# The tanh of a u tile written to its place in SBUF instead of back into its bank

## The reference

```
proj = hidden_states @ W_in.T
u, gate = split(proj, 2, axis=-1)                   # 2048 channels each
u = silu(causal_conv(u, conv_w, 4 taps) + conv_b)
ssm_p = u @ Wx.T  ->  dt, B, C, each normed
delta = softplus(dt @ Wdt.T + dt_bias)
state = exp(delta * A) * state + (delta * u) * B    # over 512 steps, 16 states a channel
y = (sum over states of state * C + u * D_param) * silu(gate)
x = layernorm(x + y @ W_out.T)
```

## Time and profile before

| what | value |
|---|---|
| median of 3 runs | 2404.43 us (2392.73 to 2404.64) |
| the profiled execution's own time | 2413.77 us |
| its span (first to last instruction) | 2412.0 us |
| busy: TensorE | 2168.1 us (90%) |
| busy: VectorE | 2090.4 us (87%) |
| busy: GpSimd | 1802.3 us (75%) |
| busy: ScalarE | 1495.7 us (62%) |
| mean granted TensorE clock | 0.933 of 2.4 GHz |

### The profile page before, as it was taken

One profiled execution on the slowest core, in us unless ns is written; L12 is line 12 of the kernel. 1 busy time (PEld: TensorE's weight loads), 2 busy tenths in 40 slices (PEclk: granted clock), 3 DMA queues, 4 the chain that ended last, 5 costly groups with the idle time before them and its releaser, 6 DMA issues.

```text
span 2412.0 us, 30712 instructions
## 1 busy us (share of the span) xinstructions
PE 2168.1 (90%) x10528; PEld 1591.5 (66%) x10528; DVE 2090.4 (87%) x2462; ACT 1495.7 (62%) x2133; POOL 1802.3 (75%) x769
## 2 busy tenths in 40 slices
PE   8998688797879979989989998989999998898987
PEld 6767567576755547778875566767875567665555
DVE  4558899999989999999989998999969998999732
ACT  4388677676665565667676667665586568565421
POOL 4378889799689987967768986887678986588500
PEclk9989789899879988999989999989999999898999
DMA  4466566455323334666443434465463335353313
GB/s 149 138 211 214 188 212 198 140 195 179 101 66 95 109 113 141 210 213 199 158 158 107 108 118 132 138 230 170 134 195 98 108 114 183 107 169 104 82 57 122
DMA packets 152651, 353.52 MB, mean 147 GB/s; under 512 B 17776, under 2 KB 27376, under 8 KB 152496
## 3 DMA queue, kind: packets, MB, share of 16 engines
q1 hardware_dynamic: 152496, 351.56, 45.8%
HBM read 282.65 MB, written 68.85 MB: 146 GB/s over the span
## 4 chain that ended last, share of the span: by engine, by line
PE 50%; DVE 27%; issue 9%; ACT 7%; POOL 2%; DVEq 0%; ACTq 0%; POOLq 0%
PE state_t L767 13%; DVE drive L906 13%; PE bank L816 13%; DVE y_acc L914 6%; PE bank L793 5%; PE bank L795 5%; PE bank L794 5%; DVE scratch L921 2%; PE bank L767 2%; ACT decay L1142 2%; POOL drive L1307 1%; ACT L1142 1%; DVE ln_stats L989 1%; PE bank L861 1%; ACT rows L1244 1%
## 5 line engine op out<-in xcount | busy, mean ns | idle before, releaser
L1307 POOL TENSOR_TENSOR drive<-delta_u,b_bcast 128x2048 f32<-128x2048 f32 x256 | 1170.5, 4574 | 154.7 <-PE state_t L767 152.8
L906 DVE TENSOR_TENSOR_SCAN drive<-decay,drive 128x512 f32<-128x512 f32 x1024 | 1193.1, 1204 | 73.6 <-ACT decay L1142 50.3
L1142 ACT ACTIVATE decay<-delta,a_sb 128x512 f32<-128x512 f32 x1024 | 692.9, 688 | 394.2 <-DVE drive L906 390.0
L767 PE MATMUL state_t<-identity,drive 128*128 128x128 f32 x4096 | 618.9, 292 | 163.8 <-DVE drive L906 120.6
L767 PEld LDWEIGHTS state_t<-identity,drive 128*128 128x128 f32 x4096 | 510.9, 150 | 375.3 <-DVE drive L906 175.7
L793 PE MATMUL bank<-cols_high,w_split 128*128 128x512 f32 (+1 forms) x1280 | 551.8, 431 | 13.0 <-POOL w_split L1332 8.7
L914 DVE SCALAR_TENSOR_TENSOR y_acc<-state_t,c_rows,y_acc 128x512 f32<-128x512 f32 x711 | 506.2, 735 | 63.3 <-PE state_t L767 60.2
L795 PE MATMUL bank<-cols_high,w_split 128*128 128x512 f32 (+1 forms) x1280 | 513.7, 401 | 0.0
L794 PE MATMUL bank<-cols_low,w_split 128*128 128x512 f32 (+1 forms) x1280 | 512.6, 400 | 0.0
L816 PE MATMUL bank<-channels,w_raw 128*128 128x512 f32 x960 | 454.7, 598 | 0.0
L1312 POOL TENSOR_TENSOR y_acc<-y_acc,scaled 128x512 f32<-128x512 f32 x249 | 319.7, 1284 | 180.0 <-ACT scaled L1162 178.2
(11 more groups left out here) (154 smaller groups left out, 1424.9 us busy)
## 6 DMA issues: line engine op xcount, KB each, us to landing
w_split<-w_split SPq DMA_DIRECT2D x288, 512.0 KB, 3.8
b_bcast<-b_rows SPq DMA_DIRECT2D x256, 256.0 KB, 3.5
w_raw<-in_w_out SPq DMA_DIRECT2D x128, 256.0 KB, 2.9
w_raw<-in_w_in SPq DMA_DIRECT2D x96, 256.0 KB, 4.2
gates<-scratch SPq DMA_DIRECT2D x64, 256.0 KB, 3.8
scratch<-gates SPq DMA_DIRECT2D x64, 256.0 KB, 4.5
rows<-in_x_rows SPq DMA_DIRECT2D x4, 2048.0 KB, 8.6
out<-rows SPq DMA_DIRECT2D x16, 512.0 KB, 4.9
```

The lines of the kernel that those rows point to most:

```text
L767: last = engine.transpose(bank[0:tile.shape[1], i * P:(i + 1) * P], tile, identity[:, :])
L906: engine.tensor_tensor_scan(state, decay[(GT * s + t) % DECAYS][:, :], state, 0.0, ALU.mult, ALU.add).then_inc(signal["scan"])
L1142: engine.activation(decay[i % DECAYS][:, :], delta[:, g % 2, t, :], ACT.Exp, scale=a_sb[:, j, n:n + 1]).then_inc(signal["decay"])
L1307: engine.tensor_tensor(drive[key % DRIVES][:, :, :], du[:, :, :], row, ALU.mult).then_inc(signal["drive"])
```

## The change

The tanh of a u tile is written to the place in `channels` where u will stand, and u_silu reads it there and writes over it. The bank is given back after u_conv instead of after u_silu. The wait for the out product of sequence b-2 moves from u_silu (VectorE) to u_tanh (ScalarE), since that is now the first to write the tile. The planner's assumed duration of u_silu is 0.6 instead of 0.585.

```diff
@@ u_job, the planner's pieces @@
-        put("DVE", due + 3.5, 2.18, "u_conv", key, [("u_tap", key)])
-        put("ACT", due + 4, 0.53, "u_tanh", key, [("u_conv", key)])
-        put("DVE", due + 4.5, 0.585, "u_silu", key, [("u_tanh", key)] + ([("o_mm", (b - 2, h, DT - 1)) for h in range(HT)] if b > 1 else []),
-            give=[("bank", ("u_mm", key)), ("scratch", ("u", key))])
+        put("DVE", due + 3.5, 2.18, "u_conv", key, [("u_tap", key)], give=[("bank", ("u_mm", key))])
+        put("ACT", due + 4, 0.53, "u_tanh", key, [("u_conv", key)] + ([("o_mm", (b - 2, h, DT - 1)) for h in range(HT)] if b > 1 else []))
+        put("DVE", due + 4.5, 0.6, "u_silu", key, [("u_tanh", key)], give=[("scratch", ("u", key))])
@@ VectorE @@
-                    conv, bank = scratch[place["scratch", ("u", key)]], banks[place["bank", ("u_mm", key)]]
+                    u, conv = chan[b % 2][:, j, :], scratch[place["scratch", ("u", key)]]
                     e.wait_ge(*done("u_tanh", key))
-                    if b > 1:
-                        for h in range(HT):
-                            e.wait_ge(*done("o_mm", (b - 2, h, DT - 1)))
-                    engine.scalar_tensor_tensor(chan[b % 2][:, j, :], bank[:, :], 1.0, conv[:, :], ALU.add, ALU.mult).then_inc(signal["u_silu"])
+                    engine.scalar_tensor_tensor(u, u, 1.0, conv[:, :], ALU.add, ALU.mult).then_inc(signal["u_silu"])
@@ ScalarE @@
                 elif stage == "u_tanh":
+                    b, j = key
                     e.wait_ge(*done("u_conv", key))
-                    engine.activation(banks[place["bank", ("u_mm", key)]][:, :], scratch[place["scratch", ("u", key)]][:, :], ACT.Tanh).then_inc(signal["u_tanh"])
+                    if b > 1:
+                        for h in range(HT):
+                            e.wait_ge(*done("o_mm", (b - 2, h, DT - 1)))
+                    engine.activation(chan[b % 2][:, j, :], scratch[place["scratch", ("u", key)]][:, :], ACT.Tanh).then_inc(signal["u_tanh"])
```

## The result

The changed kernel takes 2480.6 us (median of 4 runs, 2475.6 to 2488.1) against 2404.5 for the kernel before: a ratio of 1.0335, 95% interval 1.0309 to 1.0361, 3.35% or 80 us slower by the ratio; the two medians are 76 us apart.

A forecast was written before the change was run, and what follows sets the result against it. TensorE and VectorE, waiting for each other, bound the kernel. Stalls 72, less 14 hidden, plus 5 clock, less 4 early bank, plus 1.5 for two more VectorE additions, gave 60 us on 2404.4: 2464 us, range 2428 to 2506.

The forecast's parts named there:

- What bounds: Whole kernel: TensorE (90% busy) and VectorE (87%) wait for each other; VectorE has 29.05 us idle in the three stretches.
- the stretches: 300 to 640, 1030 to 1200 and 1598 to 1720 us, where the 48 touched tiles of sequences 1 to 3 run.
- The second input: u_silu on VectorE, sequences 1 to 3: two SBUF inputs make it wait for GpSimd's instruction; 72 us, 61 to 84.
- Lost rounds: u_silu beside busy GpSimd: a stopped instruction can also wait through GpSimd's next one; 9 us for 34 tiles.
- What idle time hides: VectorE in the three stretches: idle time swallows 14 us of the waits, half of 29.
- The clock: TensorE: idle in long stalls, its clock falls and work after runs slower; 5 us more, 0 to 18.
- The early bank: TensorE's waits for a u tile's bank: release after the third convolution step gains 4 us, 0 to 8.2.
- The order: All engines: the new plan hardly moves the order, 12 out products go behind a last transpose; 0, with 12 us either side.
- The sum: Whole kernel: 72 - 14 + 5 - 4 + 1.5 = 60 us slower, predicted median 2464 us.
- Hidden stalls (A): Rival, VectorE's stalls hidden in its idle time: within 0.5% of before, 2407 us at 40 us of waits; chance 0.08.
- No stall (B): Rival, u_silu does not stop and the earlier bank is what is left: faster, 2387 us; chance 0.08.
- Stalls that breed stalls (C): Rival, most of the 34 u_silus lose another GpSimd round and TensorE's clock stays low: 2522 us; chance 0.07.

The follow-up runs named there:

- the run with half the dose: Kernel before, its order; only odd tiles have their tanh in SBUF and a u_silu with two SBUF inputs: 2434.9 us, ratio 1.0129.
- the operands alone: Kernel before, every engine's order unchanged; tanh goes to SBUF, u_silu reads two SBUF inputs, out-product wait moves too: 2473.1 us, ratio 1.0296.
- the late release: Changed kernel's order with the old operands; whoever takes the bank next waits for u_silu: 2441.1 us, ratio 1.0159.
- the memset run: Changed kernel, order and early bank release kept; u_silu's product replaced by a VectorE memset of the tile: 2428.9 us, ratio 1.0106.

## Why the prediction was right

- **What bounds.** Right. In the stretches VectorE was full, and what u_silu took there came out as length: 50.7 us more of u_silu, 46 us more of stretch. In the first 110 us u_silu stalled as well, 17.8 us for 16 tiles instead of 11.0, and the first scan began at 140.3 us in both.
- **The second input.** The mechanism was right in each part: 0.67 us where GpSimd is idle, the rest of the drive otherwise. The size was off for the changed kernel. I took 72 us (61 to 84); it measured 50.7, under my lower end. VectorE's busy time rose by 51.4 us where I had expected 60 to 90, and u_silu's mean is 1.57 us and not 1.8. With the positions of before, where I had read the waits off the trace, it measured 68.9. There the reading (75.3 us) was good; the new order puts u_silu elsewhere, where four of 48 wait over 4 us and not nine, and GpSimd's remainders add up to 54 us for the 32 that waited. I had treated the mean over positions as settled at 61 and up.
- **Lost rounds.** 9 us were allowed, none came in the changed kernel; they exist (one of 16 in the run with half the dose). The rule of the Trainium skill (SBUF — State Buffer, Who interferes with whom), by which the later instruction waits until the first is through, was nearer to this kernel than my addition; the 8.95 us in the run with half the dose shows that it is not the whole of it.
- **What idle time hides.** I took 14 us. For the operands alone the traces show 58.1 us more span for 68.9 of stall, so 11 hidden; the medians show 71, so none. Between the two lies the profiled execution of before, which is slower than its median. It is open how much was hidden.
- **The clock.** I took 5 us, 0 to 18. TensorE's mean granted clock is 0.927 to 0.931 in the four executions of the changed kernel, and 0.933 to 0.948, the median 0.943, in the 46 of the kernel before that were timed beside the last two rounds of experiments. The profiled execution of before has 0.933, so the two traces show next to nothing of this. The clock was also lower, 0.932 to 0.936, in the two runs with the new order and no long u_silu, and 0.928 to 0.936 with the operands alone in the old order. So both parts of the change go with a lower clock; what it cost was not separated from the rest.
- **The early bank.** I took 4 us, at most 8.2. The 8.2 counts waits twice, by matmul and by weight load; at most 5.7 were to be had. TensorE's waits for it went away. What it is worth in the new order shows only as the difference between 38 us with the late release and 25 with the early one, of which 9 may be the shorter memset: 4 to 13 us. But that is a gain against a plan that needs it.
- **The order: the step that failed.** I took 0 with 12 us to both sides; it cost 25 to 34. The sentence that failed is that the 12 out products behind the last turn are done "either way": they are, but behind the last turn their 11.8 us of TensorE's work come out as 12 us of length, while before it TensorE had waits that they could fill. From the last turn to the end it takes 151.7 to 152.6 us in the six kernels with 61 behind it, and 139.5 to 140.5 in the six with 49. The other 13 to 22 us were not pinned to a place: between the profiled executions of before and of the memset run lie 14.5 us of span in all, the tail among them, and what the medians have beyond that is in executions without a trace, and in the shorter memset. Part of it may be the clock; that is not shown.
- **The sum.** The stalls came out some 20 us too high and the order some 25 too low, and so 60 us were predicted and 80 measured (76 by the medians). The direction and the main cause were reasoned; that the number was this close owes something to two errors of opposite sign.
- **The rivals.** Hidden stalls (A): no, the stretches grew. No stall (B): no. Stalls that breed stalls (C): no; no u_silu of the changed kernel lost a round, and the time is 41 us under what (C) gave. The lower clock that it also named is there.

## What to carry to other kernels

Moving an operand from PSUM to SBUF can cost more than the bank is worth: where a VectorE instruction would get its second SBUF input, look at what GpSimd runs at that moment, and price the move by the rest of those instructions. Where VectorE was full, as in the three stretches here, that price came out almost whole. When a planner's list changes, count what stands behind the last piece of the long loop: here 12 products that moved there cost 12 us. A planner's assumed duration is worth trying at several values, for it moves that count by chance. And when two traces are compared, see first how far each profiled execution lies from its kernel's median; here the two were 14 us closer than the medians.

## What the runs showed of the hardware beyond that

GpSimd can be the one that waits. At 59.50 us of the changed kernel a split on GpSimd, 1.29 us elsewhere, took 2.58 while two VectorE instructions with two SBUF inputs ran one behind the other; at 1712.65 a drive that began 0.04 us before a u_silu took 5.21 instead of 4.6 us, and u_silu was not held (VectorE first, then GpSimd, in both pairs):

```profile
59.12 1.21 DVE L954 TENSOR_TENSOR lora_b_sb<-drive,lora_b_sb 64x1024 fp32r<-64x1024 f32 x1
60.26 0.68 DVE L931 SCALAR_TENSOR_TENSOR channels<-channels,scratch 128x512 f32<-128x512 f32 x1
...
57.45 1.30 POOL L1332 TENSOR_TENSOR w_split<-w_raw,w_split 128x512 fp32r<-128x512 f32 x1 [2.10 <-ACT w_split L1178]
59.50 2.58 POOL L1332 TENSOR_TENSOR w_split<-w_raw,w_split 128x512 fp32r<-128x512 f32 x1 [0.75 <-ACT w_split L1178]
...
1712.69 0.67 DVE L931 SCALAR_TENSOR_TENSOR channels<-channels,scratch 128x512 f32<-128x512 f32 x1
...
1712.65 5.21 POOL L1307 TENSOR_TENSOR drive<-delta_u,b_bcast 128x2048 f32<-128x2048 f32 x1
```

The drive had the earlier start in the trace, and yet VectorE went first. A held u_silu ends some 0.55 us after GpSimd's instruction, not the full 0.67: 5.03 - 4.48 at 319.83, 4.98 - 4.45 at 1159.17, and alike in the other 28 of the changed kernel. The tanh into SBUF takes 0.63 us where into the bank it took 0.60.
